# A 512-step recurrence on TensorE: two matmuls of 64 output rows per step in place of four of 32

## The reference, cut to what matters

```python
def _L0_attn_b_ref(x, A, B, C, gamma, beta):          # the recurrence
    xb = jnp.einsum('bsd,ed->sbe', x, B)
    def step(h, xb_t):
        h = jnp.tanh(h @ A.T + xb_t)
        y = h @ C.T
        return (h, y)
    h0 = jnp.zeros((batch, d), dtype=x.dtype)
    _, ys = jax.lax.scan(step, h0, xb)
    out = jnp.transpose(ys, (1, 0, 2)) + x
    ...                                               # layer norm with gamma, beta

x = x + _L0_attn_a_ref(_layernorm(x), ...)            # q, k, v, gains over 11 scales, shifted k and v, gate
x = x + _L0_ffn_ref(_layernorm(x), ...)               # mixture of experts, 8 x (128 -> 512 -> 128)
x = x + _L0_attn_b_ref(_layernorm(x), A, B, C, gamma, beta)
x = x + _L0_ffn_ref(_layernorm(x), ...)
```

## Time and profile before

| what | value |
|---|---|
| median of 3 runs | 1466.86 us (1463.73 to 1468.23) |
| time of the profiled execution | 1461.65 us |
| its span, first to last instruction | 1459.9 us |
| PE busy / PE weight load busy | 1129.1 / 824.4 us |
| DVE / ACT / POOL busy | 830.6 / 674.4 / 771.3 us |
| mean granted TensorE clock | 0.870 of full speed |
| recurrence on PE (L1039) | 4096 MATMUL, busy 135.7 us; 4096 LDWEIGHTS, busy 86.5 us |
| recurrence on ACT (L868) | 512 ACTIVATE, busy 93.7 us |

### The profile page before, as it was taken

One profiled execution on the slowest core, in us unless ns is written; L12 is line 12 of the kernel. 1 busy time (PEld: TensorE's weight loads), 2 busy tenths in 40 slices (PEclk: granted clock), 3 DMA queues, 4 the chain that ended last, 5 costly groups with the idle time before them and its releaser, 6 DMA issues.

```text
span 1459.9 us, 32432 instructions
## 1 busy us (share of the span) xinstructions
PE 1129.1 (77%) x9702; PEld 824.4 (56%) x9702; DVE 830.6 (57%) x1815; ACT 674.4 (46%) x2124; POOL 771.3 (53%) x1258
## 2 busy tenths in 40 slices
PE   3666647886898888988888898776998888886863
PEld 1233325554666555665555565666776677765753
DVE  4788797888677876897785778333022211313010
ACT  2233315544546544664545554344454554544431
POOL 2444475438836497467585463966416713354042
PEclk9677768998899979996879999997798798989997
DMA  4600011112111122112121112453233334434452
GB/s 125 178 1 0 1 47 50 52 54 87 51 42 54 40 66 64 52 49 71 47 83 41 46 47 62 123 144 98 90 96 101 101 88 112 115 99 132 135 154 68
DMA packets 121574, 112.01 MB, mean 77 GB/s; under 512 B 16148, under 2 KB 90685, under 8 KB 121405
## 3 DMA queue, kind: packets, MB, share of 16 engines
q1 hardware_dynamic: 110640, 92.46, 22.3%
q0 software_dynamic: 8192, 16.79, 3.8%
q10 hardware_dynamic: 2573, 0.69, 0.2%
HBM read 81.31 MB, written 28.57 MB: 75 GB/s over the span
## 4 chain that ended last, share of the span: by engine, by line
POOL 31%; PE 28%; issue 14%; DVE 13%; ACT 8%; DMA 2%; SPq 2%; ACTq 1%; DVEq 1%; POOLq 0%
POOL acc L679 10%; PE bank L1012 7%; POOL back L706 6%; POOL sorted_x L695 6%; PE bank L999 5%; POOL mom L644 5%; PE bank L1039 3%; DVE term L1196 2%; ACT hT L848 2%; DVE made L1167 2%; POOL rrs L644 2%; PE bank L906 2%; PE bank L965 1%; PE bank L938 1%; POOL prs L644 1%
## 5 line engine op out<-in xcount | busy, mean ns | idle before, releaser
L679 POOL TENSOR_TENSOR acc<-acc,term 128x512 f32<-128x512 f32 x219 | 288.5, 1317 | 63.3 <-DVE term L1196 44.5
L1012 PE MATMUL bank<-w,hT 128*128 x1584 | 274.9, 310 | 56.8 <-ACT hT L848 48.3
L999 PE MATMUL bank<-xTb,w1b 128*128 128x128 f32 x1584 | 278.8, 314 | 12.4 <-ACT xTb L836 7.2
L848 ACT ACTIVATE hT<-bank,b1T 128x128 f32<-128x128 f32 x792 | 233.1, 373 | 106.1 <-PE bank L999 100.9
L1012 PEld LDWEIGHTS bank<-w,hT 128*128 128x128 f32 x1584 | 230.2, 211 | 87.0 <-issue 80.6
L999 PEld LDWEIGHTS bank<-xTb,w1b 128*128 128x128 f32 x1584 | 236.6, 217 | 32.3 <-issue 12.2
L1303 DVE TENSOR_TENSOR ysb<-bank,b2bc 128x128 f32<-128x128 f32 x198 | 56.5, 286 | 294.1 <-PE bank L1012 279.3
L1196 DVE TENSOR_TENSOR term<-bank,V 128x512 f32<-128x512 f32 x251 | 168.3, 683 | 59.2 <-PE bank L965 36.1
L706 POOL DMA_INDIRECT back<-sorted_y,slot_i x128 | 128.7, 1006 | 126.3 <-issue 72.9
L1167 DVE SCALAR_TENSOR_TENSOR made<-bank,qkvb,K 128x512 f32<-128x512 f32 x251 | 176.0, 741 | 18.0 <-PE bank L938 8.7
L868 ACT ACTIVATE hid<-bank 128x16 f32<-128x16 f32 x512 | 93.7, 183 | 191.1 <-PE bank L1039 189.7
(11 more groups left out here) (160 smaller groups left out, 1629.8 us busy)
## 6 DMA issues: line engine op xcount, KB each, us to landing
w1b<-in_W SPq DMA_DIRECT2D x198, 256.0 KB
xsb<-sorted_x SPq DMA_DIRECT2D x198, 64.0 KB
sorted_y<-ysb SPq DMA_DIRECT2D x198, 64.0 KB
X<-in_x SPq DMA_DIRECT2D x64, 64.0 KB
out_x<-X SPq DMA_DIRECT2D x64, 64.0 KB
sorted_x<-K SPq DMA_DIRECT2D x10, 256.0 KB, 3.6
sorted_x<-xnj,slot_i POOLq DMA_INDIRECT x128
back<-sorted_y,slot_i POOLq DMA_INDIRECT x128
```

Of the source, the lines that this page charges most:

```text
L679: nc.gpsimd.tensor_tensor(acc[:], acc[:] if k > 1 else term[0][:], term[k % NTERM][:], ALU.add).then_inc(S["terms_added"], 1)
L848: last = nc.scalar.activation(tile(hT[u], c), tile(bank[4 + u], c), ACT.Gelu, bias=b1T[:, ds(e * HC + c, 1)])
L999: last = nc.tensor.matmul(tile(bank[4 + n % 2], c), tile(w1b[n % W1_RING], c), xTb[n % 2][:], start=True, stop=True, skip_group_check=True)
L1012: last = nc.tensor.matmul(bank[4 + n % 2][:, 0:D], tile(hT[n % 2], c), w2[:, ds(e * (HC * D) + c * D, D)], start=(c == 0), stop=(c == HC - 1),
```

## The change: the same product in two pieces of 64 rows

```diff
-                    for q in range(4):
-                        last = nc.tensor.matmul(bank[6 + u][32 * q:32 * q + 32, k * NB:(k + 1) * NB],
-                                                abcT[:, 32 * q:32 * q + 32], prev, start=False, stop=True,
+                    for q in range(2):
+                        last = nc.tensor.matmul(bank[6 + u][64 * q:64 * q + 64, k * NB:(k + 1) * NB],
+                                                abcT[:, 64 * q:64 * q + 64], prev, start=False, stop=True,
                                                 skip_group_check=True)
                     last.then_inc(S["step_psum"], 1)
```

## The result

The changed kernel took 1500.92 us (median of 4 runs, 1489.82 to 1505.86) against 1465.3 us before: 1.022 times as long, 95% interval 1.018 to 1.026. A second comparison gave 1.018 (1.008 to 1.028). Some executions show a lower clock and take over 1.5% longer than the fastest of the same kernel; ratios and clocks leave them out, which in the second comparison are two of the four runs of the changed kernel. The profiled execution took 1498.91 us. The kernel is slower, as forecast, but by twice the 15.4 us that the forecast named: at the upper end of the range, 0.9 us beyond it as a time (1500.9 for 1500), just inside it as a ratio (1.022 for 1500 / 1466.86 = 1.023).

A forecast was written before the change was run, and what follows sets the result against it. No engine was taken to bound the whole, though PE was busiest. Steps 25.9 us plus drains 4.9 give 30.8, half reaching the end: +15.4 on 1461.65 is 1477.0, plus 5.2 to the median: 1482, range 1468 to 1500.

The forecast's parts named there:

- How a step runs: Step matmuls on PE: strips load in parallel, one strip's load depth sets the step; width 64 adds 40 ns.
- the third rival: Step matmuls: the two 64-column halves do not load side by side; +140 ns a step, 1513 us, chance 0.07.
- The tanh: Time from a step's first load to its tanh on ACT: 0.32 to 0.36 us, at the lower clock 0.47.
- the sum: PE work added by the change: 25.9 us in the steps plus 4.9 us of drains, 30.8 us.
- Fewer instructions win: Front of each step: sending instructions on PE's queue is what is paid, 8 for 16; 1453 us, chance 0.08.
- The rule of 25 ns: Matmul starts never closer than about 25 ns; four fewer a step worth 100 ns, estimate 1441 us.
- Drains at the reductions: PE passages between steps and 32-wide reductions: width 64 drains PE at 41 places, 0.12 us each, 4.9 us.
- The share that reaches the end: How much of the 30.8 us lengthens the execution: between 11.4 us and all, half taken, +15.4 us.
- With 20%: Steps: 20% of time at the lower clock, +93 ns there and +40 otherwise; 50.6 ns x 512 steps, 25.9 us.
- The range: Whole execution: 1468 to 1500 us for 8 in 10, around a forecast of 1482.
- Hidden: Waits of PE and of the states absorb the steps' added time; under 4.4 us reach the end, chance 0.15.

The follow-up runs named there:

- kernel with the later state: Kernel before, with ACT taking an extra one-column tanh into an unread buffer ahead of each tanh, so the state is ready later; ratio 1.002.
- two of 32 with 8 instructions: Kernel before, with each step doing only output rows 0 to 63 as two matmuls of 32 columns, the other rows left out; ratio 0.995.
- kernel with the same step and no change of clock: Kernel before, with a fifth matmul of 32 columns holding zeros ahead of each step's four; 1478.3 us, ratio 1.006.
- the last kernel: Changed kernel, with each matmul streaming 48 columns in place of 16 in 27 of a chunk's 32 steps, so sums differ; ratio 1.011.
- the step of 64 + 32 + 32: Kernel before, with every step as one matmul of 64 columns and two of 32; median 1657 us against 1547, no ratio given.
- one of 64 alone: Kernel before, with each step doing only output rows 0 to 63 as one matmul of 64 columns, the rest left out; ratio 1.006.

## Why the prediction was right and wrong, point by point

- **How a step runs.** Right. A 64-wide load takes 132 ns at best (133 forecast), 2048 of them, and the next load comes at 0.22 and 0.33 us. The strips load in parallel, halves included: the third rival (no overlap, 0.33 at full clock) did not come.
- **The tanh.** Forecast +40 and +93 ns, measured +20 and +74. A strip less is worth 17 ns on that count, not 7. As at most a third of a delay of the state reaches the end (kernel with the later state), this is at most 3 us of the sum.
- **Fewer instructions win.** This rival is refuted: two of 32 with 8 instructions hold PE for 0.17, two of 64 with 8 instructions for 0.22, five of 32 with 20 for 0.23. The rule of 25 ns between two matmuls (the Trainium skill, TensorE: Matmul & The Clock Gate, "Wait — 56ns, not 53.3ns?"), by which the change would have gained, is not what this trace shows: the four matmuls of a pass, on four strips, start 7 ns apart, and the eight of a step are over in 0.26 us.
- **Drains at the reductions.** The mechanism is right to the hundredth behind a step (0.23 for 0.22). In the order on PE there are 52 such places, 22 ahead of a reduction and 30 behind one, not 41; at the forecast's 0.12 us that is 6 us of PE time. Alone they changed the time by 1.001 (0.997 to 1.004).
- **The share that reaches the end.** Half of 30.8 us was taken. The kernel with the same step and no change of clock lost 9 us, about a third of the 27 us that its steps gained (0.044 and 0.087 us at the two clocks, with the 20% of the prediction), close to the share of the steps that stood on the chain of waits (37%, 11.4 us). Its interval (3 to 15 us) reaches from a tenth to over half, so the half is not refuted; but even its upper end is only half of the 32 us that were measured.
- **The clock.** This is the term that was missing, and the step of the prediction that failed: "With 20%" took the share of time at the lower clock from before and held it fixed, for the step and, silently, for all other matmuls. The clock fell by about 0.02 (0.866 to 0.848 and 0.842), and all of PE's work got slower: PE gained 61.9 us of busy time where the sum has 30.8. A size for it comes from the last kernel, which is 0.007 to 0.011 faster than the changed one, 10 to 16 us, though it holds PE some 12 us longer, of which a third, 4 us, would reach the end. By this estimate the clock is worth about 14 to 20 us, and with the 9 us of the longer step that makes 23 to 29 of the 26 to 32 us measured. It rests on ratios taken on different chips. Among the 28 runs of before on one chip the time falls by 4.7 us for each 0.01 of clock (correlation -0.46), 9 us for 0.02: the same sign, and less. How much of the difference is scatter stays open.
- **The range.** It reached as far as the measurement because it allowed for all 30.8 us of the steps to arrive at the end. About a third did, and the rest of the loss goes with the clock, which the sum does not have. That the time lies so near the range is luck.
- **Hidden** did not come; its argument, that waits absorb part, holds for about two thirds of the step's own time.

## What to carry to other kernels

When small stationary operands are packed side by side, the width of a piece is the depth of its loads: cut the work into the narrowest pieces, or make it as wide as its neighbours on TensorE so that no drain is paid; here the width between cost on both sides. A change of a small step can come with a lower granted clock (0.866 to 0.848 and 0.842 here), and all other matmuls then pay: read the mean time of groups that were not touched, and the clock over several runs, before the loss is put down to the edited line. A state that is ready later costs little where the order has other work between two steps (0.07 us in each of 512 steps: 1.002). And count a step from the work ahead of it, not from its own first instruction: one matmul of 128 beat both kernels (0.993 of before), and its tanh, 0.11 us later from the step's first load, is 0.085 us earlier from the matmul ahead.

## What the runs showed of the hardware

- Drains between widths: at full clock a narrower piece behind a matmul of 128 columns starts to load 0.203 us after that matmul's start, which is its 0.107 us of streaming and some 0.096 more; a load of the same width starts after 0.007. Behind a narrower piece the drain is some 0.10 us, worked out from the next load at 0.185 us. It comes between 32 and 128, 64 and 128, and 64 and 32 alike: the step of 64 + 32 + 32 holds PE for 0.39 us, which is 0.218 (one of 64 alone) plus 0.172 (two of 32).
- With 48 columns streamed in place of 16 through each matmul of 27 of 32 steps the mean granted clock was 0.862, for 0.842 to 0.848 in the kernels with 16, and the kernel was faster (1.011 for 1.018 to 1.022), though each of these steps was longer.
- The result of several strips reaches ACT 17 ns later for each strip (0.290 us with two of 32, 0.323 with four), more than the 7 ns between their starts.
